# A four-block sequence kernel: eight gate steps move to GpSimd, three normalisations to ScalarE, in a new order

## The reference

```python
x = _layernorm(x + _L0_attn_ref(x, W_q, W_kv, W_o))          # a: spectra
x = _layernorm(x + _L0_ffn_ref(x, ...))                      # g: gated experts
x = _layernorm(x + _L1_attn_ref(x, W_qkv, W_o))              # b, e: attention
x = _layernorm(x + _L1_ffn_ref(x, W_fc, W_proj))             # c: hidden layer
```

```python
score = (einsum('nds,bntd->bnts', select_weight, x_diff) ** 2).sum(-1)  # x_diff has norm 1
gate = sigmoid(imp_slope * (score - imp_center))             # 8 experts
sel_scale, sel_idx = gate.max(axis=1), gate.argmax(axis=1)
out = (1 - sel_scale) * x + sel_scale * (bias[sel_idx] + degen_up)
```

## Time and profile before

| | |
|---|---|
| median of three runs | 789.01 us |
| the profiled execution | 790.19 us |
| its span | 788.2 us |
| instructions | 14764 |
| output stores | 16, the first at 235.75 us, the 13th at 720.86 us, the last at 785.8 us |
| longest kinds of waits | POOL for the statistics, ACT for PE's scores, POOL for the squares |

### The profile page before, as it was taken

How to read it: one execution, slowest core, us unless ns; L and a number is a source line. 1 busy time by engine, 2 the same in 40 slices (tenths; PEclk the granted TensorE clock), 3 DMA queues, 4 the chain that set the end, 5 groups by cost and what they waited for, 6 DMA issues and landing times.

```text
span 788.2 us, 14764 instructions
## 1 busy us (share of the span) xinstructions
PE 667.5 (85%) x5100; PEld 525.6 (67%) x5100; DVE 588.1 (75%) x1416; ACT 474.9 (60%) x958; POOL 347.2 (44%) x537
## 2 busy tenths in 40 slices
...
GB/s 205 67 2 13 14 102 70 138 50 128 26 138 36 147 25 145 29 135 41 136 37 138 35 131 34 133 50 101 76 91 73 94 69 110 68 134 16 14 13 14
DMA packets 298170, 60.57 MB, mean 77 GB/s; under 512 B 237352, under 2 KB 293616, under 8 KB 298096
## 3 DMA queue, kind: packets, MB, share of 16 engines
...
...
## 4 chain that ended last, share of the span: by engine, by line
PE 35%; DVE 29%; SPq 13%; DMA 7%; POOL 7%; issue 6%; ACT 4%; POOLq 0%; DVEq 0%; ACTq 0%
SPq L752 10%; DVE nmax L1606 9%; PE pB L960 4%; DMA kT<-qk_scratch 4%; PE pA L944 4%; PE pC L1083 3%; PE pO L1012 3%; DMA qk_scratch<-qk_part 3%; PE pA L837 3%; PE pA L855 3%; PE pC L1061 3%; PE pA L890 3%; PE pS L986 2%; DVE spec L1448 2%; PE pS L1036 2%
## 5 line engine op out<-in xcount | busy, mean ns | idle before, releaser
L1606 DVE TENSOR_REDUCE nmax<-pB 128x2 f32<-128x512 f32 x256 | 165.7, 679 | 34.8 <-PE pB L960 34.2
L1229 ACT ACTIVATE pt<-pS 128x512 f32<-128x512 f32 x256 | 147.7, 605 | 61.1 <-PE pS L986 60.7
L960 PE MATMUL pB<-kT,qT 96*128 96x256 bf16 x512 | 90.5, 278 | 25.8 <-DVE nmax L1606 16.9
L1776 POOL TENSOR_TENSOR hsum<-hsum,hsq 128x512 f32<-128x512 f32 x48 | 64.7, 1348 | 59.5 <-ACT hsq L1269 59.3
L986 PE MATMUL pS<-qT,kT 98*128 98x256 bf16 x512 | 86.5, 276 | 4.5 <-ACT pt L1229 3.4
L1799 POOL TENSOR_TENSOR hid_lo<-hh,hid 128x512 fp32r<-128x512 f32 x64 | 84.3, 1316 | 5.3 <-ACT hh L1279 5.0
L960 PEld LDWEIGHTS pB<-kT,qT 96*128 96x128 bf16 x512 | 38.3, 98 | 59.5 <-DVE nmax L1606 39.5
L1061 PE MATMUL pC<-x3T,w1T 128*128 128x256 f32 x256 | 71.5, 312 | 7.2 <-ACT hr L1257 5.6
L1012 PE MATMUL pO<-pt,v_ext 128*32 128x256 f32 x1024 | 68.5, 385 | 4.6 <-ACT pt L1229 4.5
L1721 POOL TENSOR_SCALAR vea<-mva 128x2 f32<-128x2 f32 x16 | 3.6, 223 | 147.8 <-DVE mva L1405 147.7
L1083 PE MATMUL pC<-w2T,hid 128*128 128x256 f32 x256 | 65.3, 295 | 0.3 <-DVE ms L1661 0.3
...
## 6 DMA issues: line engine op xcount, KB each, us to landing
...
```

What stands on the lines that cost most here:

```text
L960: ins = pe.matmul(pB[h % 2][:, s * T:(s + 1) * T], qT[k][0:STACK, u * P:(u + 1) * P], kT[k][0:STACK, h * T:(h + 1) * T], start=True, stop= ...
L1229: act.activation(pt[:, (h // 4) % 2, h % 4].rearrange("p s n -> p (s n)"), pS[h % 2][:], ACT.Exp, scale=HD ** -0.5).then_inc(S["probs"], 1)
L1606: dve.tensor_reduce(nmax[:, h * SIDES:(h + 1) * SIDES], pB[h % 2][:].rearrange("p (s k) -> p s k", s=SIDES), AX.X, ALU.max, negate=True).t ...
L1776: pool.tensor_tensor(hsum[:], hsum[:], hsq[:], ALU.add).then_inc(S["hsum_done"], 1)
```

## The change

Work changes its engine in two places, and the order of all steps is new. Eight instructions of the gate leave DVE for POOL, in three steps: g_terms (the squares and the added norm), g_score (product, centre, slope) and g_pick (two_less, the one-hot row times the value, the mix). DVE keeps the bias, the reductions, the reciprocals, the comparisons and the product with desc, in g_gate1_0, g_gate1_1 and g_gate2_0 to 5. The one semaphore gate_step becomes ten, one for each hand-over. a_norm1, g_norm2 and e_norm move to ACT as an activation Identity with scale rs and bias -m * rs a side; for that POOL computes two more instructions a normalisation, the negated mean and its product with rs. a_mean, g_mean and e_mean on DVE wait for POOL's last reading, the POOL step for ACT's. ORDER, FILL and DRAIN are new for all engines; the five turns in the middle stay. In the diff below the old gate lines, are left out, and g_pow2 and e_pow get what a_pow1 gets.

```diff
@@ ORDER: the old lists @@
-    "b_max_13:+2 b_max_14:+2 e_outt_0:+2 b_max_15:+2 e_outt_1:+2 a_proj_1 c_ms:+2 b_maxt_t:+2 e_ont:+2 "
-    "a_cum:+1 e_vt:+1 e_wo:+2 g_mixt:+1 c_y:+2 e_score_0:+1 e_score_1:+1 g_mix:+1 e_score_2:+1 a_prt:+1 "
-    "e_score_3:+1 c_x3t:+1 e_score_4:+1 a_attn:+1 e_out_0:+1 e_score_5:+1 e_score_6:+1 w_turn_1:+2 "
-    "c_hid_0:+1 e_score_7:+1 e_score_8:+1 c_hid_1:+1 g_x1t e_out_1:+1 e_score_9:+1 e_score_10:+1 g_gate "
-    "e_score_11:+1 b_max_0:+1 b_max_1:+1 a_xt:-1 c_hid_2:+1 b_max_2:+1 e_score_12:+1 g_x2t:+1 b_max_3:+1 "
-    "e_out_2:+1 b_max_4:+1 e_score_13:+1 b_max_5:+1 g_qkv_0:+1 w_turn_0:+1 e_score_14:+1 b_max_6:+1 "
-    "c_hid_3:+1 b_max_7:+1 g_qkv_1:+1 b_max_8:+1 a_proj_0:-1 e_score_15:+1 b_max_9:+1 b_max_10:+1 "
-    "g_qkv_2:+1 b_max_11:+1 b_max_12:+1 w_gate e_out_3:+1 "
...
-    "c_lo_3:+1 c_hsum:+1 e_pow:+1 c_rms:+1 a_pow1 g_pow2 c_pow:+1 a_root_0:-1 a_root_1:-1 a_root_2:-1 "
-    "a_root_3:-1 c_norm:+1 a_root_4:-1 c_lo_0 c_add_1 c_lo_1 c_add_2 c_lo_2 c_add_3 "
-
-    "g_v_out:+3 g_v_in:+3 w_load_proj:+2 c_store:+3 g_out_0:+2 b_rows:+2 g_out_1:+2 w_load_fc:+1 "
-    "g_in_0:+2 w_load g_out_2:+2 g_in_1:+2 g_in_2:+2 p_load "
@@ ORDER: the new lists @@
+    "b_max_0:+1 b_max_1:+1 e_out_2:+1 b_max_2:+1 a_xt:-1 e_score_13:+1 b_max_3:+1 c_hid_2:+1 b_max_4:+1 "
+    "e_score_14:+1 w_gate:+1 w_turn_0:+1 g_qkv_0:+1 b_max_5:+1 b_max_6:+1 a_proj_0:-1 c_hid_3:+1 "
+    "e_score_15:+1 b_max_7:+1 b_max_8:+1 g_qkv_1:+1 b_max_9:+1 b_max_10:+1 e_out_3:+1 b_max_11:+1 "
+    "g_qkv_2:+1 b_max_12:+1 e_outt_0:+1 b_max_13:+1 e_outt_1:+1 b_max_14:+1 a_proj_1:-1 b_max_15:+1 "
+    "e_ont:+1 c_ms:+1 a_cum b_maxt_t:+1 e_wo:+1 w_turn_1:+2 c_y:+1 e_score_0 e_score_1 a_prt g_mixt "
+    "e_score_2 e_vt e_score_3 a_attn c_x3t e_score_4 e_out_0 e_score_5 e_score_6 g_mix e_score_7 "
+    "e_score_8 c_hid_0 e_out_1 g_x1t:-1 e_score_9 e_score_10 c_hid_1 g_gate:-1 e_score_11 g_x2t "
+    "e_score_12 "
+
+    "e_exp_2:+2 e_exp_3:+2 g_mixt_sb:+2 c_x3t_sb:+2 e_exp_4:+2 e_exp_5:+2 e_exp_6:+2 e_out_sb_0:+2 "
+    "e_exp_7:+2 e_exp_8:+2 a_norm1:+2 c_relu_0:+2 a_squares:+1 g_x1t_sb:+1 e_exp_9:+2 g_norm2:+2 "
+    "e_exp_10:+2 w_qkv_hi_0 e_out_sb_1:+2 e_exp_11:+2 c_h_0:+2 c_hi_0:+2 c_hsq_0:+2 c_relu_1:+2 "
+    "w_qkv_hi_2:+1 g_x2t_sb:+2 e_exp_12:+2 c_h_1:+2 w_cast_0:+1 a_xt_sb c_hi_1:+2 c_hsq_1:+2 e_exp_13:+2 "
+    "c_relu_2:+2 w_turn_sb_0:+2 e_exp_14:+2 c_h_2:+2 g_qkv_sb_0:+2 e_out_sb_2:+2 c_hi_2:+2 c_hsq_2:+2 "
+    "e_exp_15:+2 c_relu_3:+2 g_qkv_sb_1:+2 c_h_3:+2 a_proj_sb_0 c_hi_3:+2 c_hsq_3:+2 w_qkv_hi_1 "
+    "e_out_sb_3:+2 g_exp:+1 g_qkv_sb_2:+2 g_first:+2 w_cast_1:+2 w_unspec_sb a_proj_sb_1 e_ont_sb:+2 "
+    "g_mid:+2 e_exp_0:+1 w_turn_sb_1:+3 e_exp_1:+1 a_prt_sb:+1 e_vt_sb:+1 e_norm:+2 "
+
+    "a_spectra_1:+1 b_max_read_10:+2 b_max_read_11:+2 g_gate2_0:+1 g_gate2_1:+1 b_max_read_12:+2 "
+    "e_outt_den_0:+2 e_outt_norm_0:+2 e_outt_den_1:+2 b_max_read_13:+2 e_outt_norm_1:+2 b_max_read_14:+2 "
+    "b_max_read_15:+2 w_sign_1_3:+3 g_gate2_2:+1 b_maxt_0:+2 w_scale_1:+2 w_sign_0_1:+1 c_ms_read:+2 "
+    "b_maxt_1:+2 g_gate2_3:+1 b_maxt_sb:+2 g_rest:+2 g_gate2_4:+1 a_even:+1 g_gate2_5:+1 e_res:+2 "
+    "w_sign_0_2:+1 a_cross:+1 e_bn:+2 a_products_0:+1 a_products_1:+1 w_gate_prod w_qkv_split_0 e_mean:+2 "
+    "g_low:+2 w_sign_1_0:+2 c_res:+2 c_bn:+2 w_sign_1_1:+2 w_qkv_split_1 c_mean:+2 a_res1:+1 a_bn:+1 "
+    "w_sign_0_3:+1 c_x3t_lo:+1 a_mean:+1 g_res2:+1 g_bn:+1 g_mean:+1 a_sums g_gate1_0 w_qkv_split_2 "
+    "b_max_read_0:+1 w_bias:+1 b_max_read_1:+1 b_max_read_2:+1 g_x2t_lo:+1 b_max_read_3:+1 w_scale_0 "
+    "b_max_read_4:+1 a_xt_lo:-1 g_gate1_1 w_sign_1_2:+2 a_inverse b_max_read_5:+1 b_max_read_6:+1 "
+    "a_spectra_0 b_max_read_7:+1 b_max_read_8:+1 b_max_read_9:+1 w_sign_0_0 "
+
+    "c_lo_2:+1 c_add_3:+1 c_lo_3:+1 c_hsum:+1 c_rms:+1 g_pick e_pow:+1 c_pow:+1 c_norm:+1 a_pow1 g_pow2 "
+    "a_root_0:-1 a_root_1:-1 a_root_2:-1 c_lo_0 a_root_3:-1 g_terms:-1 a_root_4:-1 c_add_1 g_score:-1 "
+    "c_lo_1 c_add_2 "
+
+    "g_in_0:+4 g_out_2:+4 g_in_1:+4 g_in_2:+4 w_load_fc:+3 w_load c_store:+4 p_load:+2 w_load_proj:+3 "
+    "g_v_out:+4 g_v_in:+4 g_out_0:+3 b_rows:+3 g_out_1:+3 "
...
+            def norm(r, rs, nb, done):
+                for s in range(SIDES):
+                    act.activation(r[:, s, :], r[:, s, :], ACT.Identity, bias=nb[:, s:s + 1], scale=rs[:, s:s + 1]
+                                   ).then_inc(done, 1)
+
+            def a_norm1(i, k):
+                act.wait_ge(S["a_pow"], nth(i, PER["a_pow"], 1))
+                norm(x1[k], rsa, nba, S["x1_done"])
+
+            def g_norm2(i, k):
+                act.wait_ge(S["g_pow"], nth(i, PER["g_pow"], 1))
+                norm(xr[i % RESID], rsg, nbg, S["x2_done"])
+
+            def e_norm(i, k):
+                act.wait_ge(S["e_pow"], nth(i, PER["e_pow"], 1))
+                norm(xr[i % RESID], rsb, nbb, S["x3_done"])
...
-            def norm(r, mv, rs, done):
-                for s in range(SIDES):
-                    dve.tensor_scalar(r[:, s, :], r[:, s, :], mv[:, s, 0:1], rs[:, s:s + 1],
-                                      ALU.subtract, ALU.mult).then_inc(done, 1)
...
             def a_mean(i, k):
                 dve.wait_ge(S["a_moments"], nth(i, PER["a_moments"], 2))
+                if has(i):
+                    dve.wait_ge(S["a_pow"], before(i, PER["a_pow"]))
                 mean(mva, sta, S["a_var"])
...
...
+                else:
+                    dve.wait_ge(S["gate_terms"], nth(i, PER["gate_terms"], 2))
                     dve.tensor_reduce(gt[:, 0], f2[:].rearrange("p s (e k) -> p s e k", k=SEL), AX.X,
...
+                                      ALU.add).then_inc(S["gate_ratio"], 1)
+                    dve.reciprocal(gt[:, 2], gt[:, 1]).then_inc(S["gate_ratio"], 1)
 
             def g_gate2(i, n):
                 if n == 0:
                     dve.wait_ge(S["gate_exp"], nth(i, PER["gate_exp"], 1))
...
+                    dve.tensor_scalar(gt[:, 6], gt[:, 5], 1.0, None, ALU.add).then_inc(S["gate_sum"], 1)
                 elif n == 1:
...
+                    dve.wait_ge(S["gate_sum"], nth(i, PER["gate_sum"], 1))
+                    dve.tensor_reduce(low, gt[:, 6], AX.X, ALU.min).then_inc(S["gate_sum"], 1)
                 elif n == 2:
...
+                    dve.wait_ge(S["gate_sum"], nth(i, PER["gate_sum"], 2))
+                    dve.tensor_tensor(gt[:, 9], gt[:, 6], each(low), ALU.is_equal).then_inc(S["gate_marks"], 1)
+                    dve.reciprocal(sel, low).then_inc(S["gate_sel"], 1)
                 elif n == 3:
...
+                    dve.wait_ge(S["gate_marks"], nth(i, PER["gate_marks"], 1))
+                    dve.tensor_tensor(gt[:, 9], gt[:, 9], both(desc), ALU.mult).then_inc(S["gate_marks"], 1)
                 elif n == 4:
...
+                    dve.wait_ge(S["gate_marks"], nth(i, PER["gate_marks"], 2))
+                    dve.tensor_reduce(first, gt[:, 9], AX.X, ALU.max).then_inc(S["gate_first"], 1)
                 else:
...
+                    dve.wait_ge(S["gate_first"], nth(i, PER["gate_first"], 1))
+                    dve.tensor_tensor(gt[:, 10], both(desc), each(first), ALU.is_equal).then_inc(S["gate_one"], 1)
 
             def g_res2(i, k):
+                dve.wait_ge(S["gate_rest"], nth(i, PER["gate_rest"], 1))
...
             def a_pow1(i, k):
+                if has(i):
+                    pool.wait_ge(S["x1_done"], before(i, PER["x1_done"]))
+                apart(pool)
                 pool.wait_ge(S["a_var"], nth(i, PER["a_var"], 2))
                 apart(pool)
+                pool.tensor_scalar(nma[:].rearrange("p (s a) -> p s a", a=1), mva[:, :, 0:1], -1.0, None, ALU.mult
+                                   ).then_inc(S["a_eps"], 1)
                 plus_eps(vea, mva, S["a_eps"])
-                pool.wait_ge(S["a_eps"], nth(i, PER["a_eps"], 1))
-                root(rsa, vea, S["a_pow"])
+                pool.wait_ge(S["a_eps"], nth(i, PER["a_eps"], 2))
+                root(rsa, vea, S["a_rs"])
+                pool.wait_ge(S["a_rs"], nth(i, PER["a_rs"], 1))
+                pool.tensor_tensor(nba[:], nma[:], rsa[:], ALU.mult).then_inc(S["a_pow"], 1)
...
+            def g_terms(i, k):
+                pool.wait_ge(S["gate_read"], nth(i, PER["gate_read"], 1))
+                pool.wait_ge(S["x1_sq"], nth(i, PER["x1_sq"], 2))
+                pool.tensor_tensor(f2[:], f[:, :, 0:G_M], f[:, :, 0:G_M], ALU.mult).then_inc(S["gate_terms"], 1)
+                pool.tensor_tensor(gt[:, 1], f[:, :, G_M:G_U], each(s2[:]), ALU.add).then_inc(S["gate_terms"], 1)
+
+            def g_score(i, k):
+                pool.wait_ge(S["gate_ratio"], nth(i, PER["gate_ratio"], 2))
+                pool.tensor_tensor(gt[:, 3], gt[:, 0], gt[:, 2], ALU.mult).then_inc(S["gate_score"], 1)
+                pool.wait_ge(S["gate_score"], nth(i, PER["gate_score"], 1))
+                pool.tensor_tensor(gt[:, 3], gt[:, 3], both(center_sb[:]), ALU.subtract).then_inc(S["gate_score"], 1)
```

(22 more changed lines are left out.)

105 lines of the change are left out of this document (33 added, 72 removed), and 575 rows, old and new, of tables (DRAIN, FILL, ORDER).

## The result

The changed kernel takes 791.1 us (median of 20 runs, 789.4 to 797.0). Beside the kernel before on the same chip the ratio is 1.0055, 95% interval 1.0034 to 1.0075: slower by half a percent, where 0.9% faster was forecast. The profiled execution took 791.37 us, its span 789.6 us (before 790.19 and 788.2).

The account below looks back on a forecast made before the run. PE, 93% busy in the middle stage, was taken as the bound, its idleness as nearly all there was to win. -11.0 (middle) + 2.5 (fill) + 1.2 (drain) = -7.3 us gave 782 us, range 767 to 798.

Parts of the forecast that it names:

- DVE's waits: Middle stage: of 21.6 us that PE waits for DVE, 2.4 stay, a gain of 19.2 us.
- ACT's waits: Middle stage: normalisations on ACT make PE wait between scores, net 0.68 us an element, 8.2 us in twelve.
- Transfers: Middle stage: PE's 6.3 us of waits for transfers were let stand, no change.
- The middle stage as one sum: Twelve elements between output stores: -19.2 + 8.2 = -11.0 us, with PE's clock granted in full.
- Fill: Before the first output store: longer normalisations +2.3, gate chain +1.2, 1.0 taken back; +2.5 us, bounds -3 and +6.
- Drain: At the end: e_norm, twice on the path, costs 0.6 us each; +1.2 us, bounds -2 and +4.
- POOL at 24.6 us an element, never the bound: POOL's busy time with gate steps and normalisation extras rises from 20.7 to 24.6 us an element, 61%.
- The signs: Middle stage: L1606 waits under 4 us, new ACT waits 13 us, DVE 28 us an element, period about 39.5 us.
- A: Full gain: ACT's additions are free and DVE's waits go whole, 766 to 771 us; chance 0.18.
- B: ACT bounds the score phase, up to 3.04 us an element, deciding from 1.3; up to 810 us; chance 0.17.
- C: DVE waits for POOL's g_terms ahead of maximum reads, the 21.6 us stay, 793 us; chance 0.16.
- D: Identity needs another ACT table, two loads a pair, 123 us on top, 905 us; chance 0.02.

Follow-up runs that it names:

- e11: e5's kernel (changed kernel, two DVE entries moved behind b_max_read_15@9) with ACT normalising only the first 128 of 256 columns; 778.2 us.
- e2: Changed kernel with the three normalisations back on DVE, without POOL's negation and product, the gate's steps staying on POOL; 786.6 us.
- e6: Changed kernel with normalisations back on DVE, x3's right behind its mean in the last four elements, and two DVE entries moved behind b_max_read_15@9; 778.5 us, ratio 0.9884.
- e3: Changed kernel with the gate's steps and the normalisations both back on DVE, so only the order differs from the kernel before; 816.0 us.
- e5: Changed kernel with two DVE entries, a_spectra_1@12 and g_gate2_2@11, moved once behind b_max_read_15@9; 789.8 us.
- e9: Changed kernel with POOL's long steps c_add and c_lo cut to 64 of 512 columns, the rest of both results left out; 778.5 us.

## Why the prediction was wrong, point by point

*The bound.* Right: PE's waits were what there was to win, and they fell. Twelve turns had 31.41 us of PE idleness before and 22.53 after: -8.9 us, against -11.0 forecast. (The forecast cut at output stores, I cut at c_y; the turns are the same work, one element each.)

*DVE's waits, -19.2.* Mis-sized: over the twelve turns they went from 20.1 to 8.3 us, -11.8. I let 2.4 us stand, and 8.3 did. "DVE's two-input steps lose up to a microsecond" to POOL, I had read from the earlier trace rows, and then reckoned as if the loss left with the steps that left: other DVE steps now stand beside POOL (889 and 854 ns), and they made the stall. DVE's busy time fell to 29.2 us an element, not 27.9.

*ACT's waits, +8.2.* Measured +8.4 (4.2 to 12.6 us) over the twelve turns. The size is right by luck: the step that I priced at 431 ns from the square in the earlier trace rows takes 594 ns. Six times 0.16 us are 1.0 us more of ACT an element, and the 1.52 us that I added for two pairs were 2.18. The row was of the wrong form: the square has no operand per partition, this one has a scale and a bias. The Trainium skill (ScalarE: Activation LUTs, What ACT_TABLE_LOAD costs) had the price: 186 ns + 0.833 ns an element, and some 93 ns for each pointer operand. By it I estimate 585 ns for this step and 479 for the halved one of e11; the traces agree, at 591 to 596 and 485 to 490 ns.

*Transfers, 0.* Measured -6.0 (6.0 to none in these turns): a gain that I did not forecast. (The three terms give -9.4; the difference to -8.9 is rounding and waits too short to be listed.)

*The middle stage as one sum.* This is the step that failed. I worked out an average turn and multiplied it by twelve, with the clock "granted in full" throughout. Six turns bore it out (0.94 us against 0.92), in part by luck: there the waits for DVE fell by 8.0 us and not 9.6, and those for transfers by 1.2 and not 0. The other six lie in and behind the seam of the lists, whose new order I checked for depth but not for who is late there. Two stalls were followed by two stretches at half the clock, and PE's busy time rose by 6.6 us in the last six turns (6.5 in all twelve), a term that the sum had at nothing. -8.9 + 6.5 = -2.4 us were measured instead of -11.0.

*Fill, +2.5.* Measured +2.97, but not made up as forecast. e2 and e6, with DVE's normalisations, reach element 0's c_y at 211.9 and 211.7 us, the changed kernel at 215.8: the normalisations' share is some 3.9 us, not 2.3. The gate's +1.2 us don't show: e2, with the gate on POOL, is 0.9 us ahead of the kernel before, and 3.2 ahead of e3, which has the gate on DVE. And e11, with the same chain, is at 212.0. The sum's nearness is luck. The first output store, which the forecast had 2 to 3 us later, is issued at 230.59 us, 5.2 earlier: in SP's new list it stands ahead of a load and the two v transfers that it stood behind, so it doesn't measure the fill. *Drain, +1.2.* Measured +0.84 behind element 12's c_y. *POOL at 24.6 us an element, never the bound.* Right on the busy time (24.1). *The signs.* PE's waits for the maxima fell from 14.9 to 4.9 us (forecast: under 4), those for ACT came to 12.6 (13), and a turn takes 39.58 us on average (39.5).

*The sum.* -8.9 + 6.5 + 3.0 + 0.8 = +1.4 us, as the spans say, where -7.3 was forecast.

*Rivals.* None of the four is what happened. A fell with DVE's waits. B's mechanism is there at the forecast's price, 0.7 us an element, and not at 1.3. C: no wait of DVE for g_terms shows among its waits. D: one table load in the whole trace, so Identity needs none; what the Trainium skill says of fillers (ScalarE: Activation LUTs, Table sets: the hidden batching unit) agrees. The rival that was missing is a stall that brings the clock down: its price is not the wait alone (1.8 us of idleness in the seventh turn) but the slow work behind it too (3.0 us).

*Still open:* why the clock falls behind some stalls and not behind others (in the changed kernel waits of 1.19 us at 660 and 1.26 us at 670 brought no fall, one of 0.97 us at 686 did), and why repairing one of them (e5) is followed by a fall elsewhere; what part of e9's gain is the end of the interference; what brought e11's fill forward; what made the moves slow on the old lists; what the gate's steps cost DVE at the best places in its list.
